# A macaron block with a six-layer local transformer: the attention's token shift made in a copy, and three orders changed

## The reference

```python
x = x + 0.5 * F(layernorm(x))
x = x + recurrence(layernorm(x))          # w_in, a scan over time, w_out
x = x + 0.5 * F(layernorm(x))

def F(x):
    for i in range(6):
        x = attn_layer(shift_tokens(x), Wqkv[i], q_scale[i], k_scale[i], Wo[i]) + x
        x = ffn_layer(shift_tokens(x), ln_g[i], ln_b[i], W1[i], b1[i], W2[i], b2[i]) + x
    return x

def shift_tokens(t):
    a, s = jnp.split(t, 2, -1)
    s = jnp.pad(s, ((0, 0), (1, 0), (0, 0)))[:, :-1]
    return jnp.concatenate([a, s], -1)
```

## Time and profile before

| what | value |
|---|---|
| median of 3 runs | 3380.83 us (3379.4 to 3381.69) |
| the profiled execution's own time | 3380.69 us |
| its span, first to last instruction | 3378.9 us |
| mean granted TensorE clock | 0.994 |
| TensorE matmul / weight load busy | 3288.9 us (97%) / 2482.8 us (73%) |
| VectorE busy | 2758.7 us (82%) |
| ScalarE busy | 2424.5 us (72%) |
| GpSimd busy | 2227.0 us (66%) |
| input shift (`xs<-Z`, both uses) | 4 x 384 transfers of 32, 28, 3.8 and 0.2 KB |
| identity matrix | 64 KB, 5.1 us from issue to landing |

### The profile page before, as it was taken

The page is one execution under the profiler, slowest core; times in us unless marked ns, Lnnn a source line. Parts: engine busy times, 40 slices in busy tenths (PEclk is TensorE's granted clock), DMA queues, the critical chain, the costliest instruction groups (busy, mean ns, idle before and its releaser), DMA issues. The chain is left out here.

```text
span 3378.9 us, 150942 instructions
## 1 busy us (share of the span) xinstructions
PE 3288.9 (97%) x63515; PEld 2482.8 (73%) x63515; DVE 2758.7 (82%) x6952; ACT 2424.5 (72%) x3769; POOL 2227.0 (66%) x1454
## 2 busy tenths in 40 slices
PE   6999999999999999999999999999999999999998
PEld 3777777777777777777777777777777777777776
DVE  5788888888888888889998888888888888888885
ACT  2777777777777777777777777777777777777775
POOL 4666666666666666667888666666666666666663
PEclk7999999999999999999999999999999999999999
DMA  3111111111111111111111111111111111111111
GB/s 115 51 48 51 48 48 50 48 51 47 48 46 51 48 51 48 49 49 48 50 42 51 48 50 48 48 50 48 51 45 48 48 51 48 51 48 51 50 51 42
DMA packets 199180, 170.06 MB, mean 50 GB/s; under 512 B 139610, under 2 KB 172525, under 8 KB 198509
## 3 DMA queue, kind: packets, MB, share of 16 engines
q1 hardware_dynamic: 193901, 157.05, 17.1%
q10 hardware_dynamic: 4608, 3.34, 0.3%
HBM read 33.38 MB, written 1.05 MB: 10 GB/s over the span
## 5 line engine op out<-in xcount | busy, mean ns | idle before, releaser
L1112 POOL TENSOR_TENSOR rot<-rot,swp 128x1024 f32<-128x1024 f32 x384 | 907.4, 2363 | 140.0 <-DVE rot L901 140.0
L705 ACT ACTIVATE sq<-proj 128x512 f32<-128x512 f32 x768 | 437.7, 596 | 551.2 <-PE proj L503 540.0
L503 PE MATMUL proj<-wq,xsT 128*128 128x512 f32 x1536 | 772.4, 625 | 14.4 <-DVE rot L901 10.2
L1121 POOL TENSOR_TENSOR rot<-rot,rn 128x1024 f32<-128x1024 f32 x384 | 724.4, 1908 | 0.0
L1102 POOL TENSOR_TENSOR rt<-rt,half 128x1 f32<-128x1 f32 x192 | 105.3, 548 | 807.0 <-DVE rt L971 807.0
L895 DVE TENSOR_TENSOR swp<-proj,tab 128x512 f32<-128x512 f32 x768 | 522.6, 680 | 17.0 <-ACT sq L705 13.6
L901 DVE TENSOR_TENSOR rot<-proj,tab 128x512 f32<-128x512 f32 x768 | 519.7, 677 | 1.5 <-PE tps L514 1.5
L514 PEld LDWEIGHTS tps<-idf,rot 128*128 128x128 f32 x3072 | 360.2, 141 | 207.3 <-issue 203.4
L1025 DVE SCALAR_TENSOR_TENSOR hT<-proj,b1c,fg 114x128 f32<-114x128 f32 (+1 forms) x576 | 166.7, 345 | 419.7 <-ACT fg L769 414.2
L1106 POOL TENSOR_TENSOR prob<-prob,rr 128x1024 f32<-128x1024 f32 x192 | 365.4, 1903 | 186.0 <-DVE rr L983 186.0
L540 PEld LDWEIGHTS sps<-kT,qT 64*32 64x32 f32 x24576 | 366.0, 106 | 134.8 <-issue 134.4
(11 more groups left out here) (111 smaller groups left out, 5743.0 us busy)
## 6 DMA issues: line engine op xcount, KB each, us to landing
vb<-va SPq DMA_DIRECT2D x192, 384.0 KB, 3.5
vb<-va SPq DMA_DIRECT2D x192, 128.0 KB, 3.4
wq<-in_L_ffn_Wqkv SPq DMA_DIRECT2D x95, 192.0 KB
xs<-Z SPq DMA_DIRECT2D x384, 32.0 KB
xs<-Z SPq DMA_DIRECT2D x384, 28.0 KB
xs<-Z SPq DMA_DIRECT2D x384, 3.8 KB
xs<-Z SPq DMA_DIRECT2D x384, 0.2 KB
wo<-in_L_ffn_Wo SPq DMA_DIRECT2D x94, 64.0 KB
```

Of the source, the lines that this page charges most:

```text
L503: mm(proj[:, c % 2, :], xsT[:, k.parity(L_QKV), :], wq2[:, bass.ds(w + c * 512, 512)], start=True, stop=True).then_inc(p_qkv[c], 1)
L705: fn(sq[:, c * 512:(c + 1) * 512], proj[:, c % 2, :], ACT.Square).then_inc(a_sq[c], 1)
L1112: g_.tensor_tensor(r, r, swp[:, g * INNER:(g + 1) * INNER], ALU.add).then_inc(g_add[g], 1)
L1121: g_.tensor_tensor(r, r, rn[:, g * HEADS:(g + 1) * HEADS].unsqueeze(2) .to_broadcast([P, HEADS, DH]), ALU.mult).then_inc(g_nm[g], 1)
```

## The change

- The input of the attention is no longer shifted by transfers. TensorE transposes `Z` itself, waiting for `v_z` and `m_z`. ScalarE's copy to `xsT`, which has one column more, now makes the shift: the lower 64 partitions (features) go to columns 0 to 127, the upper 64 to columns 1 to 128, and the upper half of column 0 comes from column 128 of the other buffer, scaled by 0 at the start of a sequence. The tile `xs` and its semaphores go.
- SP sends `vb` when AV's matmuls are done (`p_O`) and not when their result is copied (`a_oT`), and the weights before the shift for L_WO.
- VectorE does L1003 before chunk 3's straight product (`rotate(k, 3, False)`) and not after `rsqrt(k, 4)`. It still waits for `p_wo` and `a_xn`; for `d_xs` it waits no more, but for `p_xT`.

```diff
--- before.py
+++ after.py
@@ -88,8 +88,7 @@
         mask = sb("mask", [2 * 512], BF16)
         idf = sb("idf", [P])
         idb = sb("idb", [P], BF16)
-        xs = sb("xs", [2, P])
-        xsT = sb("xsT", [2, P])
+        xsT = sb("xsT", [2, 1 + P])
         xs2 = sb("xs2", [P])
         xn = sb("xn", [P])
         xnT = sb("xnT", [P])
@@ -137,7 +136,6 @@
         d_mask = sem("d_mask")
         d_raw, d_mlp, d_late = sem("d_raw"), sem("d_mlp"), sem("d_late")
         d_wq0, d_wq, d_wo = sem("d_wq0"), sem("d_wq"), sem("d_wo")
-        d_xs = [sem(f"d_xs{g}") for g in range(2)]
         d_xs2 = sem("d_xs2")
         d_vb = sem("d_vb")
         d_out = sem("d_out")
@@ -448,29 +446,20 @@
 
                     for lag in (L_X, L_WO):
                         k.slot(lag), k.slot(lag, 0, P // 2), k.slot(lag, 1, P // 2)
-                if k.on(L_X):
-
-
-                    k.wait(v_z, L_X)
-                    k.wait_mid(m_z, TILES)
-                    if k.reg is None:
-                        k.wait(p_xT, L_X + 2)
-                    shift(k, L_X, xs[:, k.parity(L_X), :], d_xs[k.parity(L_X)])
                 if k.on(L_SM):
 
 
-                    if k.reg is None:
-                        k.wait(a_v[0], L_SM)
-                    k.wait(a_oT, L_SM + 1)
+                    k.wait(a_v[0], L_SM)
+                    k.wait(p_O, L_AV)
                     par = k.parity(L_SM)
                     sp.dma_start(vb[WIN:P, :], va[0:P - WIN, par, :]).then_inc(d_vb, 16)
                     sp.dma_start(vb[0:WIN, :], va[P - WIN:P, 1 - par, :]).then_inc(d_vb, 16)
+                load_weights(k)
                 if k.on(L_WO):
 
 
                     k.wait(v_z1, L_WO)
                     shift(k, L_WO, xs2[:, :], d_xs2)
-                load_weights(k)
                 if k.reg is None and k.s >= OUT:
                     t = k.s - OUT
                     sp.wait_ge(f_out, t + 1)
@@ -500,13 +489,13 @@
             def project(k, c):
 
                 w = k.layer_parity(L_QKV, 3 * INNER)
-                mm(proj[:, c % 2, :], xsT[:, k.parity(L_QKV), :],
+                mm(proj[:, c % 2, :], xsT[:, k.parity(L_QKV), 0:P],
                    wq2[:, bass.ds(w + c * 512, 512)], start=True, stop=True).then_inc(p_qkv[c], 1)
 
             def values(k, c):
 
                 w = k.layer_parity(L_S, 3 * INNER)
-                mm(proj[:, c, :], xsT[:, k.parity(L_S), :], wq2[:, bass.ds(w + (4 + c) * 512, 512)],
+                mm(proj[:, c, :], xsT[:, k.parity(L_S), 0:P], wq2[:, bass.ds(w + (4 + c) * 512, 512)],
                    start=True, stop=True).then_inc(p_v[c], 1)
 
             def transpose_rot(g, done):
@@ -648,8 +637,9 @@
                     if k.mid(M_T) is not None:
                         k.wait_mid(m_xn, M_T)
                         tr(tps[:, 5, :], mx_n[:, :], idf[:, :])
-                    k.wait_pair(d_xs, L_X, 64)
-                    tr(tps[:, 4, :], xs[:, k.parity(L_X), :], idf[:, :]).then_inc(p_xT, 1)
+                    k.wait(v_z, L_X)
+                    k.wait_mid(m_z, TILES)
+                    tr(tps[:, 4, :], Z[:, bass.ds(k.slot(L_X), P)], idf[:, :]).then_inc(p_xT, 1)
                 if k.on(L_F):
                     k.wait(a_xnT, L_F)
                     if k.reg is None and k.s in (L_F, L_F + 1):
@@ -772,7 +762,12 @@
                 if k.on(L_X):
                     k.wait(p_xT, L_X)
                     k.wait(p_v[0], L_X + 2)
-                    cp(xsT[:, k.parity(L_X), :], tps[:, 4, :]).then_inc(a_xT, 1)
+                    hf, par = P // 2, k.parity(L_X)
+                    cp(xsT[0:hf, par, 0:P], tps[0:hf, 4, :])
+                    cp(xsT[hf:P, par, 1:P + 1], tps[hf:P, 4, :])
+                    k.wait(a_xT, L_X + 1)
+                    fn(xsT[hf:P, par, 0:1], xsT[hf:P, 1 - par, P:P + 1], ACT.Copy,
+                       scale=0.0 if k.tile(L_X) % POS == 0 else 1.0).then_inc(a_xT, 1)
                 if k.mid(M_T) is not None:
 
                     k.wait(p_xT, L_X)
@@ -989,18 +984,19 @@
                     rotate(k, 3, True)
                     k.wait(a_sq[2], L_QKV)
                     v.tensor_reduce(xsq[:, HEADS:2 * HEADS], heads(sq[:, INNER:2 * INNER]), AX, ALU.add).then_inc(v_red[1], 1)
+                if k.on(L_WO):
+                    k.wait(p_wo, L_WO)
+                    k.wait(a_xn, L_WO + 1)
+                    k.wait(p_xT, L_WO)
+                    zs = Z[:, bass.ds(k.slot(L_WO), P)]
+                    v.tensor_tensor(zs, zs, ops[:, 0, 0:P], ALU.add).then_inc(v_z1, 1)
+                if k.on(L_QKV):
                     rotate(k, 3, False)
                     rsqrt(k, 1)
                     rotate(k, 2, True)
                     rsqrt(k, 2)
                     rotate(k, 2, False)
                     rsqrt(k, 4)
-                if k.on(L_WO):
-                    k.wait(p_wo, L_WO)
-                    k.wait(a_xn, L_WO + 1)
-                    k.wait_pair(d_xs, L_WO - 1, 64)
-                    zs = Z[:, bass.ds(k.slot(L_WO), P)]
-                    v.tensor_tensor(zs, zs, ops[:, 0, 0:P], ALU.add).then_inc(v_z1, 1)
                 if k.on(L_QKV):
                     rsqrt(k, 5)
                     rsqrt(k, 7)
@@ -1046,6 +1042,7 @@
                                            op0=ALU.mult, op1=ALU.add).then_inc(f_out, 1)
 
             v.memset(kT[:, :, 2 * P:2 * P + WIN], 0.0)
+            v.memset(xsT[:, 1, P:P + 1], 0.0)
             v.memset(va[:, 1, :], 0.0).then_inc(c_zero, 1)
             dve.wait_ge(c_zero2, 1)
             for g in range(2):
```

## The result

| | before | after |
|---|---|---|
| median | 3381.26 us (4 runs, 3379.4 to 3383.32) | 3412.31 us (4 runs, 3407.77 to 3415.53) |
| the profiled execution | 3380.69 us, span 3378.9 | 3407.77 us, span 3406.0 |
| granted clock, mean | 0.994 | 0.996 |

The changed kernel takes 1.0096 times as long, interval 1.0082 to 1.0109: 31 us more. The forecast was 3430 with 3400 to 3445: the sign, the place and the mechanism were right, the rise was forecast 1.6 times too large (49.6 us).

The account below looks back on a forecast made before the run. TensorE is nearly full, in a closed cycle with VectorE's run: scores, run, value projection. 86 x 0.37 + 86 x 0.25 + 0.3 = 53.6 us, less 1 (start) and 3 (traffic), is 49.6 on 3380.69: 3430, 80% range 3400 to 3445.

Parts of the forecast that it names:

- A: Steps where ScalarE copies the carried keys: 86 of them, forecast to lose a mean of 0.37 us each.
- B: Alternate steps where ScalarE doesn't copy the carried keys: 86 of them, forecast to lose a mean of 0.25 us each.
- The sum's own time: L1003 (Wo's sum) in VectorE's run before rotation chunk 3: 0.20 us a step, upper bound 0.28.
- The wait for `xn`: Moved sum on VectorE waiting for ScalarE's L748: 0.27 us late in A, no cost in B.
- The wait for Wo: Moved sum on VectorE waiting for the Wo matmuls (L606), with 0.07 us wake-up: 0.03 us late.
- The middle: 17 steps with the second branch's work on both engines, 0.17 to 0.79 us between them: together lose 0.3 us.
- Nothing gives it back in the step: Claim that no lateness is regained: TensorE's following work is packed, VectorE's next run starts only at the scores' end.
- The shift in the copy: ScalarE's one copy to xsT becomes three: +0.47 us, hidden in 0.94 us of room before the query projection.
- The start: First transpose no longer waits for the shift until 9.68 us: -1 us, bounds -3 and +1.
- Instruction fetch: Less DMA traffic may shorten TensorE's 41.7 us of issue idle time in the scores: -3 us, bounds 0 and -42.
- Wo alone delays: Rival: the moved sum waits for Wo but xn costs nothing; +31 us, 3412; 12% chance.
- The fetches get quick: Rival: half of TensorE's 41.7 us issue idle time in the scores goes; +32 us, 3413; 12% chance.

Follow-up runs that it names:

- e6: Changed kernel with the LayerNorm statistics of xs2 moved from VectorE's run into its idle time before the gelu's product: 3408.56 us, ratio 1.0092.
- e5: Changed kernel with Wo's sum one instruction later, behind chunk 3's rotation: 3389.68 us, ratio 1.0040.
- e9: Changed kernel with two xs2 buffers, so Wo's sum waits only for the xn of a step earlier: 3391.03 us, ratio 1.0042.
- e1: Changed kernel with Wo's sum put back behind the inverse root's fourth instruction: 3370.13 us, ratio 0.9976.
- e2: Kernel before with Wo's sum alone moved in front of chunk 3's rotation: 3423.18 us, ratio 1.0134.
- e3: Kernel before with the input's shift in ScalarE's copies, without its transfers; SP's order and Wo's sum as before: 3374.46 us, ratio 0.9989.
- e4: As e3, but SP still sends the 768 removed transfers, into a tile nobody reads: 3375.86 us, ratio 0.9992.
- e11: Repeat of e4, four unread transfers a step: 3380.16 us, one run.
- e10: Repeat of e3, the shift in the copy alone: 3376.59 us, one run.
- e8: As e1, with SP held in the first three steps until the input tiles are normalised: 3371.32 us, ratio 0.9981.

## Why the prediction was right, and where its size was off

- **Where to look.** Right. The waits did not show VectorE as what bounds the step; the free distance between a rotation's end and a load did: 0.10 us in A, nothing in B. "Works without a gap" holds from the maximum on in the usual step, but e6 shows that the run has no slack to give there either: ScalarE's square is ready only 0.04 us before VectorE comes to it.
- **The signs.** The projection waited for rotation 2 191 times, the steps are 17.18 and 16.92, and no query projection waits for `xsT` behind the start. VectorE's idle time in front of the sum is there 77 times, but the profile puts it down to "issue" and not to `xn`, and at 0.17 us and not 0.27, because the instruction ahead lasts longer than its distance to the next.
- **The sum's own time.** Right by the row: the next instruction starts 0.20 us after it in both kinds, 0.08 to 0.09 before its end, and step B is 16.92, where the whole 0.28 us would have made it 17.00. The Trainium skill, "VectorE: DVE Perf Modes", section "The DRAIN you can't avoid", was read only by half: behind the rule that the next operation waits for the pipe to empty, it says that one which is not held starts earlier. So the page leaves room for the 0.20, and did not speak against it.
- **The wait for `xn`.** Right, and half of the loss: 0.27 us forecast, and 0.27 measured, the sum at 1025.48 against VectorE's readiness at 1025.21 (1024.09 + 1.12), and shown from two sides by e5 and e9. Together with the sum's own time, chunk 2 is 0.47 us late in A, exactly as forecast.
- **The wait for Wo.** Mis-sized by 0.02 to 0.03: 0.07 us of wake-up was taken from the scores, this one took 0.04 to 0.05, so VectorE hardly waits and chunk 2 is 0.21 late in B. TensorE has regained 0.01 to 0.02 of the lateness by the scores' start. So the steps grew by 0.35 and 0.20 where 0.37 and 0.25 stood: 47 us for twice 86 steps, where 53 stood.
- **The middle.** Wrong, if small: 0.3 us of loss in 17 steps was forecast. Between the changed kernel and the one before, the 25 distances there grew by only 1.2 us together, but that is a loss and a gain at once: the move alone costs 4.9 us there (434.7 in e1, 439.6 with it) and 5.0 (438.4 before, 443.3 in e2), where the forecast has some 3 (eight usual steps and the 0.3). The rest of the change gives 3.7 us back.
- **"Nothing gives it back in the step."** This failed. Steps have disturbances, and in the traces a step that waits for VectorE is partly spared them. Outside the middle, the move lengthens the other 162 distances by some 44 us, and the time from the fifth to the last scores grows by 35.8 in all (e1 to the changed kernel), 4.9 of it in the middle: 13 us come back, 6 of them in the scores' issue entry (32.7 to 26.5). From before to e2 it is 12.5, with 8 in the entry. Two profiles of one kernel differ by up to 5.5 us in this, so it is more than chance between two profiles, but not exact; by the medians, 39 to 45 us for the move, it would be 4 to 10. It is the largest error in the sum by the traces.
- **The shift in the copy.** ScalarE's +0.47 was +0.46, and it was hidden as said. The rest of the change was forecast at -4 in all, -3 of it for the missing transfers: it gave 8.1 us in the medians for all but the sum (e1), 3.8 for the copy alone (e3), and 1.4 to 3.6 for the transfers (e4 against e3, e11 against e10), which is within the spread.
- **The start.** Forecast -1, measured +2.8 in the trace (fifth scores 130.5 against 127.7). The identity matrix came at 9.57 and not at about 7:

```profile
9.57 0.47 PE L642 MATMUL tps<-idf,Z 128*128 128x128 f32 x1 [9.57 <-DMA idf<-const_ident]
...
11.44 0.26 ACT L766 COPY xsT<-tps 64x128 f32<-64x128 f32 x1
...
11.99 0.20 ACT L769 ACTIVATE xsT<-xsT 64x1 f32<-64x1 f32 x1
...
12.33 3.75 PE L492 MATMUL proj<-wq,xsT 128*128 128x512 f32 x4 [2.29 <-ACT xsT L769]
```

  The column copied at 11.99 is followed by the projection at 12.33, which was at 11.94: 0.39 of the 2.8. The rest comes up in the steps that fill the pipeline and was not followed one by one. The cause was named, the key weights sent at once, but its weight was not: e8, which holds them back, has the identity at 7.39 and the fifth scores at 127.6.
- **SP's order.** Forecast 0. e1 and e3 differ by it alone: 3370.1 and 3374.5, ten runs each, 3366 to 3376 against 3370 to 3379. A gain of some 4 us is likely from so many runs; but the two traces show none (66.7 and 66.6 above the usual step), and what would cause it stays open. It may be half of e1's 8 us.
- **Instruction fetch.** The Trainium skill, "Runtime: NRT & Kernel Launch", section "Instruction fetch mechanics", calls a block's crossing mostly hidden, by which the last term would be 0. The entries of 21 to 42 us in every kernel here are idle time in the scores with no cause shown. That these stalls are fetches was not shown, only that they change without a change in TensorE's program (e2), so no run here decides on the page.

The sum by what was measured: 44 + 5 for the move, less 13 covered, less 8 for the rest of the change (the start's 2.8 in it): 28; the medians differ by 31.

The median of 3412 is also the number of two rivals, so the number alone proves little for the mechanism. *Wo alone delays* had 3412, but its condition is false: `xn` does delay (e5, e9). *The fetches get quick* had 3413 with half of the 41.7 us gone; the entry did fall by 15, but 8 went with the move alone (e2) and 9 with the rest alone (e1). So a part of its relief is in the result, though not shown to come from fetches, and the -3 that stood for it was too small.

## What to carry to other kernels

Before an instruction is moved forward on a busy engine, list every semaphore it waits for with the time at which that comes at the new place: here the wait for `xn` cost as much as the instruction. An engine that is 97% busy can still be set by one that is 82% busy; look for the shortest distance between a producer's end and the consumer's start, not for the longest wait. And removing work ahead of a wait that another engine sets was worth nothing here (e6): find where the chain enters the engine before cutting it.

## What the runs showed of the hardware that I had not expected

- The wake-up from a matmul's end to VectorE was 0.07 us behind the scores and 0.04 to 0.05 behind Wo; from ScalarE to VectorE 0.08 to 0.10; from VectorE to TensorE 0.05 to 0.06.
- A copy of 64 partitions by 128 columns took 0.25 to 0.26 us, of 128 partitions 0.28; a single column on 64 partitions 0.20.
- TensorE's stalls in the scores changed without any change in its own program: 41.7 us before, 33.4 in e2, where it waits for VectorE in each step (one trace each; two profiles of one kernel differ by up to 5 us).
- Weights (512 KB, then twice 256 KB) whose sending began 3.2 us earlier (1.91 in e1, 5.06 in e8) delayed a 64 KB load that was needed first by 2.3 us (9.70 in e1, 7.39 in e8).
